# Context and k, v weights laid out with channels on the partitions, and a new order of blocks on every engine

## The reference

```python
q = w8a8_linear(layernorm(x), wq, bq)       # both sides rounded to int8 steps
k = cond @ wk.T + bk                        # cond (8, 256, 512), plain fp32
v = cond @ wv.T + bv
attn = softmax(q @ k.T / sqrt(32) + mask)   # per head
x = x + tanh(g_xattn) * w8a8_linear(attn @ v, wo, bo)
h = layernorm(x); qh = fp8(h)               # scaled per row
t = silu(qh @ w_gate.T) * (qh @ w_up.T)     # 1408 wide, weights rounded to fp8
x = x + tanh(g_ffn) * (fp8(t) @ w_down.T)
```

## Time and profile before

| what | value |
|---|---|
| time, median of 3 runs | 593.86 us (591.64 to 595.87) |
| span of the profiled execution, first to last instruction | 589.9 us |
| median of the runs less that span | 4.0 us |
| TensorE, VectorE, ScalarE, POOL busy | 515.7, 516.0, 471.3, 227.2 us |
| mean granted TensorE clock | 0.963 of full speed |
| first step, second step | to 67.86 us, to 127.30 us |
| steady steps | 59.20 us each, six to 482.5 us |
| tail | 482.5 to 589.9 us |

### The profile page before, as it was taken

How to read it: one execution, slowest core, us unless ns; L and a number is a source line. 1 busy time by engine, 2 the same in 40 slices (tenths; PEclk the granted TensorE clock), 3 DMA queues, 4 the chain that set the end, 5 groups by cost and what they waited for, 6 DMA issues and landing times.

```text
span 589.9 us, 10832 instructions
## 1 busy us (share of the span) xinstructions
PE 515.7 (87%) x3456; PEld 326.7 (55%) x3456; DVE 516.0 (87%) x1294; ACT 471.3 (80%) x1148; POOL 227.2 (39%) x212
## 2 busy tenths in 40 slices
PE   0778689999999999999999999999999997965843
PEld 0665466567656765676567656765676554532311
DVE  4999989989799979997999799979997996599794
ACT  4499989999898989898989898989898987783251
POOL 4315134004632463246424642464245422452420
PEclk9899989999999999999999999999999998797888
DMA  8913233011002100210021001100100000000000
GB/s 265 386 62 98 99 108 104 6 54 38 1 2 84 44 0 2 79 47 3 1 74 54 1 1 59 68 2 2 54 37 1 1 2 37 0 2 0 36 1 36
DMA packets 14024, 28.75 MB, mean 49 GB/s; under 512 B 2576, under 2 KB 4624, under 8 KB 13968
## 3 DMA queue, kind: packets, MB, share of 16 engines
q1 hardware_dynamic: 9216, 16.65, 8.0%
q0 software_dynamic: 3328, 11.41, 5.7%
q10 hardware_dynamic: 1424, 0.01, 0.1%
HBM read 23.87 MB, written 4.19 MB: 48 GB/s over the span
## 4 chain that ended last, share of the span: by engine, by line
PE 52%; DVE 26%; issue 10%; ACT 2%; DVEq 0%; POOL 0%; POOLq 0%; ACTq 0%
PE bank_s L808 8%; PE bank_t L873 7%; PE bank_u L828 5%; PE bank_g L828 5%; PE bank_a L815 4%; PE bank_g L815 4%; DVE prob L1305 4%; PE bank_o L915 3%; DVE q L1200 3%; DVE t_sb L1195 2%; DVE t_sb L1239 2%; PE bank_a L839 2%; DVE ts L1490 2%; DVE v_sb L1229 1%; PE bank_g L1049 1%
## 5 line engine op out<-in xcount | busy, mean ns | idle before, releaser
L613 ACT ACTIVATE prob<-prob,neg_max 128x256 f32<-128x256 f32 x256 | 127.4, 505 | 2.5 <-DVE neg_max L1305 2.5
L1305 DVE CUSTOM_DVE_ANT_0 prob<-bank_s,mask_sb 128x256 f32<-128x256 f32 x256 | 96.3, 419 | 13.3 <-PE bank_t L873 5.0
L624 ACT ACTIVATE probT<-bank_t 128x512 f32<-128x512 f32 x128 | 74.0, 590 | 20.5 <-PE bank_t L873 17.2
L398 POOL TENSOR_TENSOR up<-up,wgu_scale 128x512 f32<-128x512 f32 (+1 forms) x42 | 54.9, 1306 | 89.1 <-ACT up L593 89.1
L873 PE MATMUL bank_t<-ident,prob 128*128 128x128 f32 x512 | 78.5, 281 | 3.6 <-ACT prob L613 2.4
L873 PEld LDWEIGHTS bank_t<-ident,prob 128*128 128x128 f32 x512 | 59.1, 143 | 30.3 <-issue 18.4
L808 PE MATMUL bank_s<-kf,qf 32*128 32x256 f32 x512 | 73.1, 403 | 1.9 <-DVE neg_max L1305 1.9
L808 PEld LDWEIGHTS bank_s<-kf,qf 32*128 32x128 f32 x512 | 44.0, 185 | 26.1 <-issue 19.6
L413 POOL TENSOR_TENSOR x<-x,y 128x512 f32<-128x512 f32 x14 | 19.6, 1400 | 96.9 <-DVE y L1503 96.9
L408 POOL TENSOR_TENSOR up<-gate,up 128x512 f32<-128x512 f32 (+1 forms) x42 | 54.4, 1296 | 4.2 <-DVE gate L1365 1.5
L613 ACT ACTIVATION_READ_ACCUMULATOR prob<-prob,neg_max 128x1 f32 x256 | 50.4, 197 | 0.0
(11 more groups left out here) (264 smaller groups left out, 1200.7 us busy)
## 6 DMA issues: line engine op xcount, KB each, us to landing
x_in<-in_x_dram SPq DMA_DIRECT2D x8, 512.0 KB
c_in<-in_ctx_dram SPq DMA_DIRECT2D x8, 512.0 KB
out_dram<-x POOLq DMA_DIRECT2D x7, 512.0 KB, 3.2
mask_sb<-in_mask_BxSxS_ff_dram SPq DMA_DIRECT2D x8, 256.0 KB, 3.7
t_sb<-in_L_ffn_w_down_dram SPq DMA_DIRECT2D x2, 704.0 KB, 5.5
t_sb<-in_L_ffn_w_down_dram POOLq DMA_DIRECT2D x2, 704.0 KB, 5.8
kf<-in_L_xattn_wq_dram SPq DMA_DIRECT2D x1, 1024.0 KB, 11.0
probT<-in_L_xattn_wk_dram SPq DMA_DIRECT2D x1, 1024.0 KB, 13.0
```

The lines of the kernel that those rows point to most:

```text
L398: pool.tensor_tensor(up[:, c % 2, 0:w], up[:, c % 2, 0:w], wu_scale[:, off:off + w], ALU.mult).then_inc(f["u_scaled"], 1)
L613: ins = act.activation(prob[:, head_par, t, :], prob[:, head_par, t, :], ACT.Exp, bias=neg_max[:, head_par, t:t + 1], scale=-1.0, accum_ou ...
L624: act.activation(probT[:, (slot + 3) % 4, :, :].rearrange("p a b -> p (a b)"), T_BANK[(slot + 1) % 2][:, :], ACT.Copy).then_inc(s["turned_ ...
L1305: ins = dve.tensor_tensor_reduce(prob[:, hp, t, :], S_BANK[hp][:, t * L:(t + 1) * L], mask_sb[:, hb, t, :], -1.0, 3.4e38, ALU.add, ALU.min ...
```

## The change

The host hands over ctx, w_k and w_v with their last two axes swapped. `c_in` gets the shape [128, 4, 256] with channels on the partitions; the DMAs for w_k and w_v write straight into `wkT` and `wvT`. Gone are: `pro_turn` and `pro_evac` of k and v (32 transposes, 8 copies), `ctxT_turn` and `ctxT_copy` (8 transposes and 2 copies in each of 8 steps) with their semaphores. k_project_even waits for the ctx load itself. A row of the ctx load is 256 instead of 512 floats. All lists of blocks of TensorE, VectorE and ScalarE are written anew, and two of POOL's and its tail. The diff, cut to its core (of the lists of TensorE and VectorE the new ones are shown, of the old steady ones only the head; the lists of the second step, of ScalarE and of TensorE's tail are left out; there, head_score(5) now stands ahead of group_pv(5), head_turn(5), and group_pv(5) follows head_turn(6); ScalarE's first step now begins unit_mag_0(0), unit_mag(2), gate_tanhs(2), unit_copy(3), pro_round_q(0), x_centre(0)):

```diff
-    L = ctx_in.shape[1]
+    L = ctx_in.shape[2]
...
-        c_in = sb("c_in", [P, NT, C])
+        c_in = sb("c_in", [P, CC, L])
...
-        def ctxT(c):
-
-            return c_in[:, c % 2, (c // 2) * L:(c // 2 + 1) * L]
...
-        PRO = [("k", 0), ("k", 1), ("k", 2), ("k", 3), ("q", 0), ("q", 1), ("v", 0), ("v", 1), ("v", 2), ("v", 3), ("o", 0), ("o", 1)]
...
+        PRO = [("q", 0), ("q", 1), ("o", 0), ("o", 1)]
...
+            def load_weight(name, w):
+                dst = raw8[name] if name in raw8 else (wkT if name == "k" else wvT)[:, :, :]
+                sp.dma_start(dst, w.rearrange("(c p) i -> p c i", p=P)).then_inc(s[f"w{name}_loaded"], 16)
...
-                sp.dma_start(c_in[:, :, :], ctx_in[bass.ds(b, 1)].rearrange("o (t p) c -> p (o t) c", p=P)).then_inc(s["ctx_loaded"], 16)
+                sp.dma_start(c_in[:, :, :], ctx_in[bass.ds(b, 1)].rearrange("o (c p) l -> p (o c) l", p=P)).then_inc(s["ctx_loaded"], 16)
...
-                k.load(6); k.x_var(0); k.load(4); k.load(8); k.x_plus_bias(4); k.load(10); k.load(12); k.load(14)
+                k.load(6); k.x_var(0); k.load(4); k.load(8); k.load(10); k.load(12); k.x_plus_bias(4); k.load(14)
...
-                def ctxT_out(hf):
-                    act.wait_ge(s["ctxT_ps"], 2 * b + hf + 1)
-                    act.activation(c_in[:, :, hf * L:(hf + 1) * L], A_BANK[:, :].rearrange("p (c l) -> p c l", c=2),
-                                   ACT.Copy).then_inc(s["ctxT_ready"], 1)
...
-                    if name in "kv":
-                        pe.wait_ge(s[f"w{name}_loaded"], 16)
+                    pe.wait_ge(s["w8_ints"], 1 if name == "q" else 2)
+                    for o in range(2):
                         for c in range(CC):
...
-                                        ctxT(c), start=(c == 0), stop=(c == CC - 1), skip_group_check=True)
+                                        c_in[:, c, :], start=(c == 0), stop=(c == CC - 1), skip_group_check=True)
...
-                def ctxT_turn(slot):
-                    if slot == 0:
-                        pe.wait_ge(s["ctx_loaded"], 16 * (b + 1))
-                        need(pe, s["o_normed"], 2 * (b - 1))
-                    else:
-                        pe.wait_ge(s["ctxT_ready"], 2 * b + 1)
-                    for c in range(2):
-                        for lt in range(LC):
-                            ins = pe.transpose(A_BANK[:, c * L + lt * P:c * L + (lt + 1) * P],
-                                               c_in[:, lt, (2 * slot + c) * P:(2 * slot + c + 1) * P], ident[:, :])
-                    ins.then_inc(s["ctxT_ps"], 1)
...
-                        pe.wait_ge(s["ctxT_ready"], 2 * b + 2)
+                        if first_step(b):
+                            pe.wait_ge(s["wk_loaded"], 16)
+                        pe.wait_ge(s["ctx_loaded"], 16 * (b + 1))
+                        need(pe, s["o_normed"], 2 * (b - 1))
...
@@ TensorE, first step, new list @@
+                k.unit_turn(2); k.k_project_even(2); k.k_project_even(3); k.pro_turn_q(0); k.k_project_odd(2)
+                k.k_project_odd(3); k.wo_scale_turn(5); k.unit_turn(4); k.sx_turn(6); k.xT_turn(4); k.pro_turn_o(4)
+                k.xT_turn(5); k.unit_turn(6); k.q_project_0(6); k.q_project_1(7); k.first_score(11); k.unit_turn(8)
+                k.v_project_low(10); k.v_project_high(10); k.v_project_low(11); k.unit_turn(10); k.head_score(13)
+                k.head_turn(13); k.head_turn(14); k.v_project_high(11); k.unit_turn(12); k.unit_turn(14)
+                k.head_turn(15); k.head_score(15)
...
@@ TensorE, steady step, the head of the old list and the new one @@
-                k.head_turn(0); k.ctxT_turn(0); k.oqT_turn(0); k.head_score(1); k.y_project(0); k.head_turn(1)
-                k.head_turn(2); k.ctxT_turn(1); k.group_pv(1); k.k_project_even(2); k.head_score(3); k.head_turn(3)
-                k.k_project_odd(2); k.head_turn(4); k.k_project_even(3); k.xT_turn(4); k.group_pv(5)
-                k.k_project_odd(3); k.xT_turn(5); k.head_turn(5); k.head_score(5); k.x2T_turn(5); k.sx_turn(6)
...
+                k.head_turn(0); k.k_project_even(2); k.oqT_turn(0); k.group_pv(1); k.y_project(0); k.head_turn(1)
+                k.head_turn(2); k.head_score(1); k.k_project_odd(2); k.k_project_even(3); k.head_turn(3); k.head_turn(4)
+                k.head_score(3); k.k_project_odd(3); k.xT_turn(4); k.group_pv(5); k.head_score(5); k.x2T_turn(5)
+                k.head_turn(5); k.xT_turn(5); k.head_turn(6); k.up_project(5); k.gate_project(5); k.sx_turn(6)
+                k.up_project(6); k.gate_project(6); k.q_project_0(6); k.up_project(7); k.gate_project(7)
+                k.head_score(7); k.head_turn(7); k.gate_project(8); k.up_project(8); k.head_turn(8); k.gate_project(9)
+                k.head_turn(9); k.q_project_1(7); k.up_project(9); k.head_score(9); k.head_turn(10); k.gate_project(10)
+                k.up_project(10); k.group_pv(9); k.v_project_low(10); k.v_project_low(11); k.v_project_high(10)
+                k.tT_turn(11); k.head_turn(11); k.first_score(11); k.head_turn(12); k.down_project_low(12)
+                k.v_project_high(11); k.down_project_high(12); k.group_pv(13); k.head_turn(13); k.head_score(13)
+                k.tT_turn(13); k.head_turn(14); k.o_turn(14); k.down_project_low(14); k.down_project_high(14)
+                k.head_turn(15); k.head_score(15)
...
@@ VectorE, first step, new list @@
+                k.unit_scale_0(0); k.unit_scale(0); k.unit_round_0(0); k.pro_scale_q(0); k.unit_round(3); k.pro_int_q(0)
+                k.x_stats(0); k.unit_scale(2); k.unit_scale(4); k.x_scales(2); k.pro_scale_o(2); k.pro_q(0)
+                k.unit_round(5); k.bias_scale(3); k.pro_int_o(4); k.xT_low(5); k.sx_copy(7); k.pro_o(5); k.unit_scale(6)
+                k.q_scale_0(7); k.unit_round(7); k.q_scale_1(8); k.unit_scale(8); k.unit_round(9); k.head_mask(12)
+                k.head_mask(13); k.unit_scale(10); k.unit_round(11); k.head_mask(14); k.head_mask(15); k.v_evac(11)
+                k.v_evac(12); k.unit_scale(12); k.unit_round(13); k.unit_scale(14); k.unit_round(15)
...
@@ VectorE, steady step, the head of the old list and the new one @@
-                k.head_mask(0); k.head_mask(1); k.oqT_low(0); k.x_stats(0); k.y_scale(1); k.head_mask(2)
-                k.head_mask(3); k.x_scales(2); k.x2_stats(2); k.x2_centre(3); k.head_mask(4); k.x2_max(3)
-                k.head_mask(5); k.xT_low(5); k.x2_sum_0(4); k.x2_sub_0(4); k.x2_sum_1(4); k.x2_sub_1(4); k.x2T_copy(5)
...
+                k.x_stats(0); k.head_mask(0); k.head_mask(1); k.oqT_low(0); k.x_scales(2); k.y_scale(1); k.head_mask(2)
+                k.head_mask(3); k.x2_stats(2); k.x2_centre(3); k.x2_max(3); k.head_mask(4); k.head_mask(5)
+                k.x2_sum_0(4); k.x2_sub_0(4); k.x2_sum_1(4); k.x2_sub_1(4); k.xT_low(5); k.x2T_copy(5); k.head_mask(6)
+                k.head_mask(7); k.gate_scale(6); k.gate_scale(7); k.sx_copy(7); k.t_mul(7); k.q_scale_0(7)
+                k.gate_scale(8); k.t_mul(8); k.head_mask(8); k.gate_scale(9); k.t_mul(9); k.head_mask(9); k.t_scales(9)
+                k.gate_scale(10); k.q_scale_1(8); k.t_mul(10); k.t_sum_0(10); k.t_sub_0(10); k.head_mask(10)
+                k.head_mask(11); k.gate_scale(11); k.t_sum_1(10); k.t_mul(11); k.t_sub_1(10); k.t_sum_2(11)
+                k.t_mul_last(11); k.t_sub_2(11); k.t_scales(11); k.v_evac(11); k.tT_low(12); k.head_mask(12)
+                k.t_sum_0(12); k.head_mask(13); k.t_sub_0(12); k.t_sum_1(12); k.v_evac(12); k.t_sub_1(12)
+                k.y2_scale(13); k.t_sum_2(13); k.t_sub_2(13); k.head_mask(14); k.tT_low(14); k.head_mask(15)
+                k.o_norm(14); k.o_norm(15); k.o_max(14); k.o_max(15); k.o_scales(15); k.y2_scale(15)
...
@@ VectorE, tail, new list @@
+                k.head_mask(0); k.head_mask(1); k.oqT_low(0); k.y_scale(1); k.head_mask(2); k.head_mask(3)
+                k.x2_stats(2); k.head_mask(4); k.x2_centre(3); k.head_mask(5); k.x2_max(3); k.head_mask(6)
...
+                k.t_mul_last(11); e.oqT_low(0); k.t_scales(11); e.y_scale(1); e.x2_stats(2); e.x2_centre(3)
+                k.t_sub_2(11); e.x2_max(3); k.t_sum_0(12); k.tT_low(12); e.x2_sum_0(4); e.x2_sub_0(4); e.x2_sum_1(4)
+                e.x2_sub_1(4); k.t_sum_1(12); e.x2T_copy(5); k.t_sub_0(12); k.t_sub_1(12); e.gate_scale(6)
+                k.y2_scale(13); e.gate_scale(7); e.t_mul(7); k.t_sum_2(13); e.gate_scale(8); e.t_mul(8); k.t_sub_2(13)
...
+_TURNED = ('ctx_2048', 'L0_xattn_wk', 'L0_xattn_wv')
...
+        if name in _TURNED:
+            a = _np.swapaxes(a, -1, -2)
```

308 lines of the change are left out of this document (114 added, 194 removed).

## The result

The changed kernel takes 630.3 us (median of 4 runs, 629.4 to 632.1) against 593.5 us for the one before beside it: ratio 1.061, 95% interval 1.058 to 1.064. It is slower by 6%, where I had forecast 579 us, 2.5% faster. The profiled span is 627.6 us against 589.9. Ratios leave out runs more than 1.5% above the fastest of their kernel, which carry a lower granted clock; this matters in experiment 18 alone, where it takes out seven of twelve.

A forecast was written before the change was run, and what follows sets the result against it. TensorE was taken to bound steady steps, VectorE the first, ScalarE fullest in the second, none throughout the tail. Savings of 6.0 (six steps) + 5.5 (first two) + 3.5 (tail) = 15.0 us gave 579 us; 8-in-10 range 569 to 588.

The forecast's parts named there:

- with nothing net for the order: Steady steps: the new block order adds nothing, leaving 1.0 us a step from the removal; bounds 0.2 and 2.2 us.
- 0.88 + 0.19 us of TensorE: Steady step: two ctxT transpose groups gone, 0.88 us, and the wait for the ctxT copies gone, 0.19 us.
- rival B: Steady steps: VectorE's strictly ordered queue sets the period, so the six steps give nothing: 585 us; chance 0.15.
- The first two steps, 5.5 us: First step about 4 us less, from VectorE copies and order; second 1.5 less, from ScalarE copies and waits; range 2 to 9.
- VectorE's 2.76 us hole: First step: VectorE idles 2.76 us ahead of w_max; unit_round_0, moved ahead, was to fill about 2.0 us of it.
- my 0 to 2: First step: k's four groups at 1.2 GHz take 6.9 us more TensorE time, hidden in its idle time; cost 0, at most 2.
- Which way the removed transposes worked on it: First-step clock: removed transposes were taken not to have warmed the array; otherwise the first step gives 2 us less.
- The tail, 3.5 us: Tail, only reordered: 1.5 us of TensorE's wait before group_pv(5) and 2.0 of VectorE's idle time saved; range -1 to +8.
- 18.1 us from head_turn(0): Steady step: TensorE reaches x2's turn after about 18.1 us instead of 19.90, then waits about 0.5 for the last x2 subtraction.
- Rival E: Steady steps: k_project_even and x_stats lengthen the FFN loop, each step growing by up to 3.2 us: 604 us; chance 0.06.
- no bound of mine went above 592: Whole kernel: the summed bounds of the terms ran from 564 to 592 us.

The follow-up runs named there:

- experiment 18: The removal alone, with three steady-step blocks (mask, exponential, scores) moved behind x2's chain: ratio 1.003; median of all twelve runs 601.6 us.
- the removal alone: The changed layout with every engine's list of before, less the blocks that are gone, against the kernel before: 595.4 us, ratio 1.001.
- experiment 12: The removal alone with the early part of the steady lists new, up to x2's turn and its evacuation: 606.2 us, ratio 1.021.
- experiment 11: The two mends in the changed kernel: v's last half product ahead of the first down projection, and VectorE's masks, last gate_scale and y2_scale(13) moved: 608.8 us.
- experiments 15: The removal alone with VectorE's y2_scale(13), which releases GpSimd's addition, moved ahead of t's last sum: 598.5 us, ratio 1.012.
- 16: The changed kernel with only VectorE's y2_scale(13) moved behind t's last difference: 625.2 us, ratio 1.056.
- 1 to 3: Three runs: the removal alone, 595.4 us; the old layout with new second-step, steady and tail lists, 653.9; the changed kernel with old steady lists, 593.9.
- experiment 10: The changed kernel with VectorE's two masks and last gate_scale between t's product and first sum, and y2_scale(13) behind t's last difference: 611.1 us.
- experiments 13: The removal alone with VectorE's reduction of centred x cut to 64 of 512 channels, work left out: ratio 1.001 to the kernel before.
- 14: The removal alone with k projected from 3 of its 4 channel blocks on TensorE, work left out: ratio 0.994 to the kernel before.
- 17: The removal alone with both cuts, VectorE's reduction and TensorE's k projection, work left out: 586.5 us, ratio 0.988.
- 3: The changed kernel with the steady steps' lists of before on all engines, less the removed blocks: 593.9 us.
- 5 to 11: The changed kernel with old steady lists on one or two engines (718.5, 737.0, 730.4, 705.2 us), then with blocks moved (627.5, 611.1, 608.8).

## Why the prediction was wrong

**The step that failed is "with nothing net for the order".** I took 1.0 us off each steady step; they grew by 5.3 on average. Against the removal alone, the span after is longer by 39.3 us: 1.9 up to the first steady step, 33.9 in the six, 3.5 behind. Of the 33.9, 11.7 are four steps with a stretch at 1.2 GHz, each counted over the same step at full clock (62.81, for the last 61.7); 9.1 are what the two mends recover at full clock (375.8 less 366.7 in the six; 1.3 of 1.56 us a step are VectorE's). 13.1 are left with both mends in, and what they are is open: experiment 12 loses 11.5 with the new early part alone, but in other parts of the step, and experiment 11 still has 1.7 us of stretch a step that the old lists haven't. I had compared the blocks of the lists by what they do and what waits for them, and never by what runs on GpSimd at the same moment. In the lists of before three of VectorE's operations on two SBUF tensors a step meet one of GpSimd's and lose 0.9 us together; in the new list six do and lose 4.4. That such a meeting costs time is shown (experiments 15 and 16), and that the order carries the loss (1 to 3); the share of it in the whole is bounded only by experiment 10.

**"0.88 + 0.19 us of TensorE" a step.** Measured: 0.3. Of the two ctxT groups the first stood in front of a wait for ScalarE and gave 0.03 us, not 0.44. I had read TensorE's 58.96 busy us of 59.20 as a bound with VectorE 5.4 us behind. That is true over the step and false where it counts: up to x2's turn VectorE's queue runs almost without a gap too. This is rival B, whose mechanism experiments 13, 14 and 17 bear out in a milder form (two queues in balance, not one behind the other). Nothing from the six steps, as it had, was nearly right for the removal (1.8 us); the 9 us from the other stages that its 585 kept did not come.

**The first two steps, 5.5 us.** Measured 0.15 with the old lists and -1.8 with the new ones. k's first matmul started at 18.74 us, as I had said (18 to 20), and VectorE's 2.76 us hole shrank to 1.05. But the windows of the earlier trace rows, read after the change, have a granted clock of 0.83 from 32 to 67.86 us and 0.87 in the second step (1.00 and 0.97 before). That it cost these 1.8 us was not tried by itself, and neither sign nor size of them is firm: with the same first two lists the first steady step begins at 128.2 to 132.9 us in the executions profiled for experiments 1, 12, 15 and 18, and at 128.4 to 132.0 in those of the changed kernel, 3, 5 to 11 and 16. VectorE's two long meetings there (2.5 and 3.6 to 4.2 us instead of 0.16 and 1.2) are a rival for part of it, in all of the second group and in none of the first. Of k's four groups only the first ran slowly, 3.20 us from start to start where the last pair has 1.79, so the clock cost 1.4 us of TensorE there, within my 0 to 2. Which way the removed transposes worked on it no run shows.

**The tail, 3.5 us.** It became longer by 3.9 us. The sums and products of two batches are now interleaved with GpSimd's: 9.0 us of stretch behind the last steady step, against 2.0. That it is these 7.0 us and not the order itself wasn't tried by itself.

**x2's turn.** I had counted 18.1 us from head_turn(0) for TensorE and a wait of 0.5 for VectorE. TensorE does get there in 18.0 us, but waits 1.3:

```profile
257.12 0.66 PE L821 MATMUL bank_t<-ident,prob 128*128 128x128 f32 x4
257.61 1.89 PE L769 MATMUL bank_a<-c_in,wkT 128*128 128x256 f32 x8
259.34 0.60 PE L833 MATMUL bank_g<-ident,rows 128*128 128x128 f32 x4
...
276.45 0.62 PE L861 MATMUL bank_u<-ident_h,xq 128*128 128x128 bf16 x8 [1.30 <-DVE xq L1133]
```

So the turn comes 19.3 us behind head_turn(0), against 19.9 before. TensorE's count held and VectorE's wait didn't; what was lost behind the turn I had not priced.

**Rival E** had the sign, but not the mechanism: k_project_even does put oq's turn 1.3 us later, but x2's turn comes no later for it or for x_stats. The loss lies behind x2's turn, in the parts with VectorE's blocked operations and the heads that were put back. Its 604 and 0.06 were both too small; no bound of mine went above 592 for the orders, though they were the part that I had called the least certain.

## What to carry to other kernels

In hand-ordered lists a busy share of 99% on one engine does not say what its next microsecond is worth: take one queue's time away in an experiment, then the other's, then both. Price a new order by what meets on a shared port: list the operations of VectorE with two SBUF operands and see which start while a GpSimd operation runs; each such meeting can cost up to the length of the GpSimd operation (of two in a row, in the first step here), small operations with one SBUF tensor included, and swapping two blocks can remove it. In a loop, compare a mark's distance only after checking that no block has moved across the mark. And test orders as whole sets or single moved blocks; exchanging one engine's list for another version's made this kernel 12 to 17% slower than the slower of the two sets.
